# Attention output scaled on ACT and added on POOL, in place of one multiply-and-add on DVE

## The reference

```
h = _L0_tok_ref(x)                                    # frames times a 128x128 basis
h = h + _L0_attn_ref(_layernorm(h, axis=-1))
h = h + _L0_ffn_ref(_layernorm(h, axis=-1), Wq, bq, ln_g, ln_b, keys0, keys1, down, up)

def _L0_attn_ref(x):
    scores = jnp.einsum('bnd,bmd->bnm', x, x)
    attn = jax.nn.softmax(scores, axis=2)
    return jnp.einsum('bnm,bmd->bnd', attn, x)
```

## Time and profile before

| what | value |
|---|---|
| median of 3 runs | 2026.2 us (2025.46 to 2030.39) |
| the profiled execution | 2031.43 us, of which its span is 2029.6 us |
| DVE busy | 1919.0 us, 95% of the span, 15718 instructions |
| PE busy | 1632.5 us, 80% |
| POOL busy | 1433.2 us, 71% |
| ACT busy | 1232.0 us, 61% |
| granted clock of PE, mean | 0.812 of full |

### The profile page before, as it was taken

One profiled execution on the slowest core, in us unless ns is written; L12 is line 12 of the kernel. 1 busy time (PEld: TensorE's weight loads), 2 busy tenths in 40 slices (PEclk: granted clock), 3 DMA queues, 4 the chain that ended last, 5 costly groups with the idle time before them and its releaser, 6 DMA issues.

```text
span 2029.6 us, 47236 instructions
## 1 busy us (share of the span) xinstructions
PE 1632.5 (80%) x11023; PEld 1169.5 (58%) x11023; DVE 1919.0 (95%) x15718; ACT 1232.0 (61%) x3883; POOL 1433.2 (71%) x2561
## 2 busy tenths in 40 slices
PE   5577888788888888888888788888878888986667
PEld 3235566566656655665666556656656565655456
DVE  2499999999999999999999999999999999999992
ACT  3346666666666666566556766656675665665554
POOL 2247777686777767777776777777687777767775
PEclk8877888888888787888888787888888888788765
DMA  1000000000000000000000000000000000000000
GB/s 44 7 10 4 19 7 13 13 7 19 7 19 9 13 13 6 19 7 19 7 6 22 6 19 7 19 7 7 19 9 20 7 19 7 6 13 9 7 6 11
DMA packets 46669, 24.87 MB, mean 12 GB/s; under 512 B 4827, under 2 KB 46116, under 8 KB 46390
## 3 DMA queue, kind: packets, MB, share of 16 engines
q1 hardware_dynamic: 46390, 21.85, 3.9%
HBM read 11.58 MB, written 10.26 MB: 11 GB/s over the span
## 4 chain that ended last, share of the span: by engine, by line
DVE 79%; PE 11%; ACT 5%; issue 4%; POOL 1%; SPq 1%; DMA 0%; DVEq 0%; ACTq 0%
DVE idx L1071 11%; DVE idx L1078 11%; DVE hrest L1065 10%; DVE alpha L1039 10%; DVE vals L1069 7%; DVE vals L1062 7%; DVE c L1109 5%; DVE crest L1103 5%; DVE top L1106 3%; DVE top L1100 3%; PE QB L526 2%; DVE beta L1044 2%; PE FB L418 1%; PE QB L514 1%; DVE lo L1033 1%
## 5 line engine op out<-in xcount | busy, mean ns | idle before, releaser
L914 POOL TENSOR_TENSOR bw<-beta,wp 128x1024 bf16<-128x1024 bf16 x240 | 505.2, 2135 | 347.3 <-issue 171.6
L526 PE MATMUL QB<-bw,alpha 128*128 128x48 bf16 x5120 | 554.5, 277 | 106.7 <-issue 101.1
L526 PEld LDWEIGHTS QB<-bw,alpha 128*128 128x128 bf16 x5120 | 521.0, 150 | 149.2 <-issue 139.4
L749 ACT ACTIVATE WD<-QB 32x96 f32<-32x96 f32 x1280 | 307.6, 240 | 84.5 <-PE QB L526 71.6
L1039 DVE TENSOR_SCALAR alpha<-hi 128x1024 bf16<-128x1024 bf16 x640 | 274.9, 502 | 0.0
L475 PE MATMUL SC<-WK,hidT 128*128 128x512 f32 x320 | 241.0, 846 | 12.6 <-issue 11.8
L1071 DVE FIND_INDEX8 idx<-vals,sraw 128x8 uint32<-128x64 f32 x1280 | 250.6, 218 | 0.0
L1078 DVE FIND_INDEX8 idx<-vals,hrest 128x8 uint32<-128x64 f32 x1280 | 250.6, 219 | 0.0
L1065 DVE MATCH_REPLACE8 hrest<-vals,sraw 128x64 f32<-128x64 f32 x1280 | 249.6, 207 | 0.0
L1062 DVE MAX8 vals<-sraw 128x8 f32<-128x64 f32 x1280 | 169.1, 207 | 14.1 <-ACT sraw L729 14.1
L1069 DVE MAX8 vals<-hrest 128x8 f32<-128x64 f32 x1280 | 166.6, 208 | 0.0
(11 more groups left out here) (206 smaller groups left out, 3583.3 us busy)
## 6 DMA issues: line engine op xcount, KB each, us to landing
res<-h_scratch SPq DMA_DIRECT2D x80, 64.0 KB, 1.9
xin<-in_x SPq DMA_DIRECT2D x32, 128.0 KB
h_scratch<-h2n SPq DMA_DIRECT2D x32, 128.0 KB
out<-ofin SPq DMA_DIRECT2D x64, 64.0 KB, 1.5
h_scratch<-h2n SPq DMA_DIRECT2D x32, 28.5 KB
out<-ofin SPq DMA_DIRECT2D x16, 57.0 KB
xin<-in_x SPq DMA_DIRECT2D x32, 28.0 KB
xin<-in_x SPq DMA_DIRECT2D x32, 0.2 KB
```

The costliest lines, as they stand in the source:

```text
L526: last = mm(bank[:, 48 * u:48 * u + 48], alpha[:, buf, a, :, 8 * p + u], bwv[:, :, a, :, 8 * p + u], start=(a == 0), stop=(a == 1))
L749: last = A(WD[r, RING[(t - 4) % NT], :, 8 * p:8 * p + 8], blocks[r, :, :, g], ACT.Copy)
L914: last = tt(bw[:, buf, NY * i:NY * i + NY, :], beta[:, buf, :, :], wp[:, buf, i, :].unsqueeze(1).to_broadcast([128, NY, 256]), ALU.mult)
```

## The change

The three DVE instructions for each clip that multiply and add are gone. At (1, 3) ACT now writes `osc = bank * rden` in three instructions for each clip, from PSUM into the new SBUF buffer `osc`, and POOL adds `osc` and `hcs` into `h2c`, in two instructions for each clip (the first two chunks in one). DVE keeps the reciprocals. The bank is freed by `osc_full`, and POOL gives `h2c_full`.

```diff
-    READ[f"O{_b}"] = ("h2c_full", 2, _b + 1)
+    READ[f"O{_b}"] = ("osc_full", 2, _b + 1)
...
+        osc = sb("osc", [128, 2, 3, D])
...
+                if (t, p) == (1, 3):
+                    for b in range(2):
+                        bank = f_wait(act, f"O{b}", j)
+                        act.wait_ge(s["rden_full"], 2 * j + b + 1)
+                        after(act, s["h2_full"], 2 * j + b - 1)
+                        for c, (st, n) in enumerate(CH):
+                            last = A(osc[0:n, b, c, :], bank[0:n, 129 * c:129 * c + D], ACT.Copy,
+                                     scale=rden[0:n, 3 * b + c:3 * b + c + 1])
+                        last.then_inc(s["osc_full"], 1)
...
+                if (t, p) == (1, 3):
+                    for b in range(2):
+                        pool.wait_ge(s["osc_full"], 2 * j + b + 1)
+                        pool.wait_ge(s["hcs_full"], 2 * j + b + 1)
+                        tt(h2c[:, b, 0:2, :], osc[:, b, 0:2, :], hcs[:, b, 0:2, 0:D], ALU.add)
+                        n = CH[2][1]
+                        tt(h2c[0:n, b, 2, :], osc[0:n, b, 2, :], hcs[0:n, b, 2, 0:D], ALU.add).then_inc(s["h2c_full"], 1)
...
                 if (t, p) == (1, 3):
                     for b in range(2):
                         bank = f_wait(dve, f"O{b}", j)
-                        dve.wait_ge(s["hcs_full"], 2 * j + b + 1)
+                        after(dve, s["h2c_full"], 2 * j + b - 1)
                         V.reciprocal(rden[:, 3 * b:3 * b + 2], bank[:, 128:258:129])
                         n = CH[2][1]
                         V.reciprocal(rden[0:n, 3 * b + 2:3 * b + 3], bank[0:n, 386:387]).then_inc(s["rden_full"], 1)
-                        dve.wait_ge(s["rden_full"], 2 * j + b + 1)
-                        for c, (st, n) in enumerate(CH):
-                            last = V.scalar_tensor_tensor(out=h2c[0:n, b, c, :], in0=bank[0:n, 129 * c:129 * c + D],
-                                                          scalar=rden[0:n, 3 * b + c:3 * b + c + 1], in1=hcs[0:n, b, c, 0:D],
-                                                          op0=ALU.mult, op1=ALU.add)
-                        last.then_inc(s["h2c_full"], 1)
```

More of the change, by code:

```diff
@@ L238, in build @@
             kseed_full knewton kn_full kbT_full dT_full weights_ready x_full xT_copied ss1_full sv1 seed1_full
-            newton1 xn_full xnT_copied e_full rden_full h2c_full ss2_full sv2 seed2_full newton2 h2_full
+            newton1 xn_full xnT_copied e_full rden_full osc_full h2c_full ss2_full sv2 seed2_full newton2 h2_full
             hid_full hidTn_full sq_full v3_full seed3_full newton3 std_full stdT_full hidT_full
```

## The result

| | before | after |
|---|---|---|
| median of 9 runs each | 2026.2 us (2024.84 to 2030.39) | 2030.93 us (2029.37 to 2038.09) |
| ratio, 95% interval | | 1.0024 [1.0013, 1.0035] |
| profiled execution, its span | 2031.43, 2029.6 us | 2030.93, 2029.1 us |

The change costs 4.7 us: slower, as forecast, but by a third of the forecast 14.5, and just under the range (2031 to 2052). The number is on the border of what can be told from no change (0.3%).

A forecast was written before the change was run, and what follows sets the result against it. DVE was taken as the bound in the steady part, waiting for ACT's squares at (2, 1). Losses of 9.0 + 5.0 + 2.2, less 1.7 gained, made 14.5 us: 2026.2 + 14.5 = 2041 us, range 2031 to 2052.

The forecast's parts named there:

- idle time at the seed: DVE at `row_seed` of (2, 1) would wait 2 to 4 us for ACT's squares in all 14 steady pairs.
- whether ACT catches up: After (2, 1) ACT waits 3.3 us for `newton1` and 0.6 for `c2_full`, so its place at (1, 3) stays.
- the loss is neither carried on nor given back: What a pair loses at (2, 1) was to stay as it is: 14.5 us slower in all.
- What DVE saves: Four reciprocals take some 0.35 us in place of 2.07: DVE gains 1.72 and reaches `row_seed` at 5.90.
- Scalings: Six on ACT ahead of `zexp`, 0.27 us each, 1.65 us in all with waits; ends 1.05 and 1.85.
- `zexp` to the squares' end: ACT's stretch without idle time, 6.33 us, which the scalings would move by their full length.
- a sign of its being wrong: The prediction would be wrong if the time between `zexp` and the squares' end weren't 6.3 us.
- ACT's distance at (1, 3): How far `zexp` starts behind DVE's first reciprocal: 0.3, 0.7 or 1.9 to 2.5 us, taken as unchanged.
- late pairs: Three pairs with squares ending at 8.2 to 8.8 us, where DVE already waits; each loses 1.65, 5.0 us together.
- POOL's side: POOL's additions take 1.0 to 1.5 us a clip, hidden by 3 us before ACT wants `h2c`.
- the third rival: POOL's additions, slowed beside DVE's ranking, hold up the squares: 28 us more, 2069 us; chance 0.05.
- The other estimate of the prediction: From the skill's figures, one scaling takes 0.157 us and six 0.94, so the sum is 4 to 5 us.

The follow-up runs named there:

- e1: The kernel before, unchanged, profiled a second time (also called "again"): 2026.86 us, ratio 1.000.
- e2: The kernel before with five scalings of 128 columns added on ACT at (1, 3), output unread: 2032.33 us, ratio 1.0027.
- e3: The kernel before with the multiply-and-add left out on any engine; squares and the rest read `hcs`: 2025.64 us, ratio 0.9995.
- e5: e3 with the outputs of `xh` and `y` written with a step of two: 2027.74 us, ratio 0.999.
- e7: The kernel after with reciprocals before DVE's third candidate pass of (1, 3) and scalings before `ofin` on ACT: 2031.0 us, ratio 1.0006.
- e8: e7 with ACT's squares ahead of the four `hi` of (2, 0), and `xh` and `y` written with a step of two: 2031.72 us, ratio 1.0014.
- e10: The kernel after with the second clip's query statistics product and its copy moved from (3, 1) to (3, 2): 2029.75 us, ratio 1.0016.
- e15: The kernel after with ACT's squares ahead of the four `hi` of (2, 0) and the statistics moved to (3, 2): 2030.92 us, ratio 1.0003.
- e6: The kernel before with the outputs of `xh` and `y` written with a step of two: 2030.08 us, ratio 1.0001.
- e11: e3 with the second clip's statistics product and its copy moved from (3, 1) to (3, 2): 2007.19 us, ratio 0.9912.
- e9: The kernel before with the second clip's statistics product and its copy moved from (3, 1) to (3, 2): 2017.2 us, ratio 0.995.
- e13: The kernel before with each of POOL's three `bw` products split into two halves: 2045.93 us, ratio 1.0077.
- e4: The kernel after with DVE's second `row_seed` moved a quarter later in the steady part: 2062.99 us, ratio 1.0174.

## Why the prediction was wrong

The sign was right, the size was not. Per pair the forecast was -1.72 for DVE's list and +2.88 of idle time at the seed ((14.5 + 1.7) / 14 = 1.16 us of loss). The paragraph that failed is the one on whether ACT catches up: "ACT's place at (1, 3) is set after that by DVE and PE as before, and the loss is neither carried on nor given back". By its steps:

- **What DVE saves**: right. Four reciprocals take 0.27 us in all for 0.35, `row_seed` reached at 5.90 in the pair shown; -1.51 per pair against "again", -1.64 against the first trace. DVE's busy time fell by 31 us against the first trace and by 28 against e1 (1915.8), forecast 26; that this is so near is partly luck, since 6.2 of the 28 are `xh` and `y`.
- **Scalings**: 1.51 us for 1.65, 0.25 each for 0.27. The bounds held them.
- **`zexp` to the squares' end**: 714.24 - 708.05 = 6.19 for 6.33. The text had named another length there as a sign of its being wrong.
- **ACT's distance at (1, 3)**: taken as it was before, 0.7 in eight pairs, some 2.0 in three, 0.3 in three: a mean of 0.93. After the change it is 0.45 in the pair shown, and there are no late pairs. This is the largest part: 0.48 + 0.14 + 0.14 = 0.76 us, all of the difference between 2.88 and the 2.13 measured for the idle time. ACT did catch up. It comes to the scalings from its own last `WD` (705.53 + 0.98 = 706.51), and before `ofin` it stands idle for PE's `QB`, as before. But that `ofin` begins 0.73 us ahead of DVE's first reciprocal, where it was 0.45: PE's signal sets ACT's place as forecast, and it stands earlier against DVE's list than before. e2, with ACT's load alone, has much the same distance, 0.3 to 0.45 in its last ten pairs. Why PE stands earlier isn't shown.
- **"The loss is neither carried on nor given back"**: this step failed too. I had looked for ACT to meet DVE's list again and stopped there. DVE itself meets a chain whose pace it doesn't set: at (3, 3) `xh` ends with POOL's `bw`, and of what DVE lost at (2, 1), 0.44 us of each pair came back there. The other way round the masks cost 0.21 more.
- **POOL's side**: right for the additions (1.0 to 1.1 us a clip, forecast 1.0 to 1.5; no squares waited for POOL). Its reach to DVE through the port was in the third rival, at the wrong place: I asked whether POOL's new additions suffer beside DVE's ranking, and it was DVE's masks and short instructions that suffer beside POOL's old work.

The sum again, in us of 14 pairs: 16.2 forecast, -0.75 x 14 = -10.5 for the idle time, -6.2 for `xh` and `y`, +2.9 for the masks, +2.9 for the list (1.51 for 1.72) is 5.3, beside 0.39 x 14 = 5.5 measured in the pairs and 4.7 in the medians. Against the first trace of the kernel before, the pairs differ by only 0.13. The other estimate of the prediction, 4 to 5 us, meets the 4.7 by luck: it needs six scalings in 0.94 us, and they took 1.51.

**What stays open.** Mean pairs of 119.35 to 119.60 us come back in before, after, e3, e5, e7, e8, e10 and e15, whose DVE lists differ by up to 1.8 us (e1, e6 and e2 lie beside them, at 119.2, 119.3 and 119.8). The two ties explain why DVE's list doesn't set it; what sets this length in the chain of PE, ACT and POOL, I haven't settled. The places where PE's granted clock is low are drawn along with the pair. In the last ten pairs of the changed kernel, of 119.4 to 119.5 us each, the clock goes from 2.4 to 1.2 GHz at 9.4, 53.8, 81.1 and 98.2 us of every pair, to within 0.1 us. In the last ten of e15, of the same length, it does so at seven other places, again the same in each. In the kernel before the places move from pair to pair, and the pairs take 118.9 to 120.0 us. So a rival stands beside the two ties: that the clock's lows hold the pair at this length, and `xh` and the seed only take up what is left. No run changes the clock by itself, so whether the lows hold the pair or follow it is open. Nor was it tried to take POOL's `bw` off the shared port.

## What to carry to other kernels

An engine that is busy for 99.7% of a stretch isn't thereby the bound: part of its busy time can be a wait inside an instruction. Compare the duration of the same small instruction over the span (`xh`: 0.17 us unheld, 0.95 and 1.37 held), and look for what ends when it ends. Before moving work off such an engine, list every place where it meets a chain it doesn't drive: here the gain lasted to the first of them, and so did part of the loss. And leave out the operation altogether in one run (e3) before working on where to put it; it tells how much there is to win in that kernel: 0 us here, and 10 once the statistics were moved (e11).

## What the runs showed that I had not expected

- DVE is held inside an instruction by a running one of POOL, for `tensor_scalar` from SBUF of f32 to f32 and of int32 to int32 alike: 0.17 us unheld; `xh` 1.37 in the pair shown and 1.44 in the mean in e9, `y` 2.17 behind a whole product and 1.20 behind a half (e13). A step of two in the output doesn't avoid it (e5).
- Eight masks of 128x1024 bf16 take 2.77 us alone and 6.22 beside four kinds of POOL's sums and products (e4).
- A POOL product of 128x1024 bf16 takes 2.13 us, one of 128x512 1.16.
- ACT from PSUM with a column as scale: 0.25 us for 128 columns, start to start; `ofin`, without one, 0.17.
- The same eight f32 products on PE: 2.30 us in a stretch of granted clock 0.89, 3.69 in one of 0.69, in kernels that differ only in when the reciprocals and scalings run; and in a kernel whose pairs repeat, the lows lie at the same place in each pair.
